# Attention scores in three memory banks used in turn by head, and a ring of four banks for everything else

## What is computed

```
x = x + 0.5 * attention(layernorm(x), W_gate, W_qkv)
x = x + recurrence(layernorm(layernorm(x)), ...)       # gates, a scan over time, W_out, W_skip
x = x + 0.5 * attention(layernorm(x), W_gate, W_qkv)   # the same weights again

attention: 2048 tokens, 256 features, 16 heads of 16
  every token picks one head for keys and values (argmax of the gate softmax):
  k_shared, v_shared [2048, 16]; all 16 query heads use them
  y = softmax(causal(q k_shared^T / 4)) v_shared
```

## Time and profile before

| | |
|---|---|
| median of three runs | 1090.59 us (1089.08 to 1090.8) |
| the profiled execution | 1086.89 us, span from first to last instruction 1085.2 us |
| PE / DVE / ACT / POOL busy | 990.2 / 820.7 / 751.6 / 267.3 us |
| granted TensorE clock, mean | 0.899 of full speed |
| exponentials (line 924) | 640, 594.5 us, 985 ns each on average |
| maxima (line 1050) | 960, 601.0 us, 683 ns each on average |

### The profile page before, as it was taken

One profiled execution on the slowest core, in us unless ns is written; L12 is line 12 of the kernel. 1 busy time (PEld: TensorE's weight loads), 2 busy tenths in 40 slices (PEclk: granted clock), 3 DMA queues, 4 the chain that ended last, 5 costly groups with the idle time before them and its releaser, 6 DMA issues. The chain is left out here.

```text
span 1085.2 us, 17469 instructions
## 1 busy us (share of the span) xinstructions
PE 990.2 (91%) x6546; PEld 335.9 (31%) x6546; DVE 820.7 (76%) x1448; ACT 751.6 (69%) x984; POOL 267.3 (25%) x497
## 2 busy tenths in 40 slices
PE   8897999989989899989998999989899989999986
PEld 6433332222332322223333342323242222222322
DVE  1676787798849798977864878877869898989731
ACT  2347467748667466877856867767838747888896
POOL 1226322221152201133123222521202210210324
PEclk9887599879999996989997989889989868999999
DMA  4110010000100100000010001000010000000000
GB/s 146 50 50 1 1 36 15 2 1 2 50 1 2 50 1 1 2 1 1 2 49 1 2 18 33 2 20 1 2 42 8 2 21 1 1 2 1 3 8 33
DMA packets 20228, 17.92 MB, mean 17 GB/s; under 512 B 4128, under 2 KB 20144, under 8 KB 20144
## 3 DMA queue, kind: packets, MB, share of 16 engines
q1 hardware_dynamic: 19328, 16.00, 4.8%
q10 hardware_dynamic: 816, 0.80, 0.2%
HBM read 10.24 MB, written 6.29 MB: 15 GB/s over the span
## 5 line engine op out<-in xcount | busy, mean ns | idle before, releaser
L1050 DVE TENSOR_REDUCE mxp<-ps_x 128x1 f32<-128x512 f32 (+2 forms) x960 | 601.0, 683 | 132.0 <-PE ps_x L1266 128.3
L924 ACT ACTIVATE probs<-ps_s,e_scale 128x1024 f32<-128x1024 f32 (+3 forms) x640 | 594.5, 985 | 142.3 <-PE ps_s L1289 138.8
L1266 PE MATMUL ps_x<-k_tl,q_t 48*128 48x512 f16 (+2 forms) x1792 | 346.3, 323 | 34.3 <-DVE mxp L1050 18.6
L1299 PE MATMUL ps_o<-probs,v_l 128*32 128x512 f32 (+3 forms) x2560 | 322.8, 581 | 6.3 <-POOL probs L737 5.0
L1289 PE MATMUL ps_s<-q_t,k_tl 50*128 50x512 f16 (+3 forms) x1280 | 269.1, 373 | 25.7 <-ACT probs L924 20.0
L1266 PEld LDWEIGHTS ps_x<-k_tl,q_t 48*128 48x128 f16 x1792 | 115.1, 99 | 316.2 <-DVE mxp L1050 228.2
L737 POOL TENSOR_SCALAR_AFFINE_SELECT probs<-probs 128x256 f32<-128x256 f32 x256 | 102.9, 410 | 228.4 <-ACT probs L924 227.6
L752 POOL TENSOR_SCALAR_AFFINE_SELECT d_sb<-d_sb 128x1024 f32<-128x1024 f32 x64 | 69.4, 1092 | 264.9 <-ACT d_sb L915 260.5
L1289 PEld LDWEIGHTS ps_s<-q_t,k_tl 50*128 50x128 f16 x1280 | 67.6, 96 | 185.7 <-ACT probs L924 141.5
L915 ACT ACTIVATE d_sb<-ps_x 128x512 f32<-128x512 f32 x128 | 71.0, 599 | 37.8 <-PE ps_x L1266 34.7
L1299 PEld LDWEIGHTS ps_o<-probs,v_l 128*32 128x32 f32 x2560 | 53.3, 111 | 101.4 <-issue 79.8
(11 more groups left out here) (111 smaller groups left out, 492.6 us busy)
## 6 DMA issues: line engine op xcount, KB each, us to landing
q_t<-q_scratch SPq DMA_DIRECT2D x96, 64.0 KB, 2.2
q_scratch<-q_part SPq DMA_DIRECT2D x16, 256.0 KB, 2.1
x_sb<-in_L_attn_x_dram SPq DMA_DIRECT2D x4, 512.0 KB, 8.6
out_dram<-x_sb SPq DMA_DIRECT2D x4, 512.0 KB, 2.9
q_t<-m_row SPq DMA_DIRECT2D x64, 4.0 KB
wqkv_n<-in_L_ffn_W_qkv_dram ACTq DMA_DIRECT2D x1, 768.0 KB, 6.5
w_in_sb<-in_L_attn_W_in_dram SPq DMA_DIRECT2D x1, 384.0 KB, 5.2
w_skip_sb<-in_L_attn_W_skip_dram SPq DMA_DIRECT2D x1, 256.0 KB, 4.6
```

Source lines behind the costliest of these rows:

```text
L924: a_.activation(probs[:, s % NB, 2 * hp:2 * hp + 2, P * i:QW], ps_s[hp][:, :, P * i:QW], ACT.Exp, scale=e_scale[:, 0:1]).then_inc(s_exp, 1)
L1050: v_.tensor_reduce(mxp[:, heads[0] % 2, h0:h1, tiles[0]:tiles[-1] + 1:i_step, slot], bank_of(e)[:, :].rearrange("p (h i k) -> p h i k", i= ...
L1266: last = mm(bank[:, col:col + w], q_rows(ROWS_X, c, g, hh, i * P, P), k_cols(ROWS_X, hh, l, key // P, w), start=True, stop=True)
L1299: last = mm(ps_o[VW * hh:VW * hh + VW, P * i:QW], v_l[:, l, kt, :], probs[:, s % NB, hh, P * i:QW], start=j == 0, stop=j == key_tiles(c) - 1)
```

## The change

- **Scores.** `ps_s` is one tile of three banks (`SB = 3`). Head `h` of step `s` uses bank `(4 s + h) mod 3`. A step has three score events and three exponentials: heads 0 and 1 together, then 2, then 3, and in every third step 0, then 1 and 2 together, then 3 (`GROUPS`), since a pair must lie in neighbouring banks. PE waits for the exponential of the head three before.
- **Ring.** `RING = 4`.
- **Exponential's scale.** Queries and keys are scaled so that the scale is the number `SCALE / LIFT ** 2`. The factors are now from the largest row norm of the weights: squares, two reductions, and a fourth root and two square roots on POOL (`roots`). `M_SCALE` goes from 256 to 32768.
- **Opening.** DVE copies the weight blocks out of PSUM in place of ACT, and computes the norms after the last of them. In `FIRST_WORK` the gate weights and the statistics come first, both turns of the first chunk stand ahead of `range`, and the gate product between the two `range` events.
- **Statistics.** DVE adds EPS and negates the mean; POOL has two instructions fewer.
- **Planner.** Two halves of the array are followed each for itself, side events depend on what they need in place of the last side event, costs are changed, and `SIDE_WORK` has other steps.
- POOL masks a diagonal step in three instructions in place of two.

```diff
-RING = 3
+RING = 4
-M_SCALE = 256.0
+M_SCALE = 32768.0
+IN_RANGE, LIFT = 40000.0, 0.125
+GROUPS = [[(0, 2), (2, 1), (3, 1)], [(0, 2), (2, 1), (3, 1)], [(0, 1), (1, 2), (3, 1)]]
+SB = 3
+PER_STEP = len(GROUPS[0])
+def group(s, k):
+    return GROUPS[s % SB][k]
-FIRST_WORK = [("weights", r) for r in range(6)] + [("wgate",)] + prepare(0, 0)
-FIRST_WORK[8:8] = [("range", 0), ("range", 1)]
-SIDE_WORK = [(-23, -10, prepare(0, 1)), (9, 9, [("bias",)]), (9, 40, prepare(0, 2)), (57, 57, prepare(0, 3)),
-             (60, 65, branch(0)), (81, 81, prepare(1, 0)), (117, 140, branch(1)), (140, 140, prepare(1, 1)),
-             (140, 158, branch(2)), (164, 174, prepare(1, 2)), (180, 203, branch(3)), (210, 214, prepare(1, 3))]
+FIRST_WORK = [("wgate",), ("stats", 0, 0)] + [("weights", r) for r in range(6)] \
+    + [("norm", 0, 0), ("turn", 0, 0, 0), ("turn", 0, 0, 1), ("range", 0), ("gate", 0, 0), ("range", 1)] \
+    + prepare(0, 0)[5:]
+SIDE_WORK = [(-38, -25, prepare(0, 1)), (10, 10, [("bias",)]), (10, 24, prepare(0, 2)), (57, 60, prepare(0, 3)),
+             (63, 63, branch(0)), (81, 84, prepare(1, 0)), (113, 140, branch(1)), (140, 140, prepare(1, 1)),
+             (140, 157, branch(2)), (165, 180, prepare(1, 2)), (180, 203, branch(3)), (210, 210, prepare(1, 3))]
-EXP, EXP_COLUMN = 150, 1.66
+EXP, EXP_COLUMN = 65, 0.83
...
-        if e[0] in SIDE_KINDS and e[0] not in ("kv", "q", "skip"):
-            t = max(t, self.side_end)
-        return t
+        return max([t] + [ended[x] + back for x in needs(e)])
...
-        ps_s = [pb(f"ps_s{i}", [P, 2, QW]) for i in range(2)]
+        ps_s = pb("ps_s", [P, SB, QW])
...
+        def scores_of(s, k):
+            first, heads = group(s, k)
+            at = (GH * s + first) % SB
+            return ps_s[:, at:at + heads, :]
...
-                    a_.activation(probs[:, s % NB, 2 * hp:2 * hp + 2, P * i:QW],
-                                  ps_s[hp][:, :, P * i:QW], ACT.Exp, scale=e_scale[:, 0:1]).then_inc(s_exp, 1)
+                    a_.activation(probs[:, s % NB, first:first + heads, P * i:QW], scores_of(s, k)[:, :, P * i:QW],
+                                  ACT.Exp, scale=SCALE / LIFT ** 2).then_inc(s_exp, 1)
...
+                v_.tensor_scalar(var[:, :], mv[:, :, 1], EPS, None, ALU.add)
+                v_.tensor_scalar(neg[:, :], mv[:, :, 0], -1.0, None, ALU.mult).then_inc(s_var, 1)
+            def loading(e):
+                r = e[1]
+                dve.wait_ge(s_fill, filled(e))
+                v_.tensor_copy(wqkv_t[:, :, r * P:(r + 1) * P],
+                               bank_of(e)[:, 0:DC * P].rearrange("p (a h) -> p a h", a=DC)).then_inc(s_rd, 1)
+                if r == 5:
+                    own(v_.tensor_tensor(squares, rows, rows, op=ALU.mult))
+                    own(v_.tensor_reduce(w_rows[:, :], squares, axis=AX, op=ALU.add))
+                    v_.tensor_reduce(w_part[:, :], w_rows[:, :].rearrange("p (a r) -> p a r", a=2), axis=AX,
+                                     op=ALU.max).then_inc(s_norms, 1)
...
+                    own(v_.tensor_copy(w_ratio[:, 1:3], bank[:, 0:2]))
+                    own(v_.reciprocal(w_inv[:, :], w_ratio[:, 1:3]))
+                    v_.tensor_tensor(w_ratio[:, 0:1], w_ratio[:, 1:2], w_inv[:, 1:2], op=ALU.mult)\
+                        .then_inc(s_norms, 1)
+                    dve.wait_ge(s_root, 1)
...
-                    if s:
-                        pe.wait_ge(s_exp, 2 * (s - 1) + hp + 1)
+                    past = GH * s + first + heads - 1 - SB
+                    if past >= 0:
+                        pe.wait_ge(s_exp, exp_of(past))
```

More of the change, by code:

```diff
@@ L157, in weights @@
     if e[0] == "max":
-        beside = e[2] % 2 and past == ("max", e[1], e[2] - 1)
-        return 15 if beside else 226, "rows", [("ACT", 480) if on_diagonal(e) else ("DVE", 600)]
+        return 226, "rows", [("ACT", 480) if on_diagonal(e) else ("DVE", 600)]
     if e[0] == "warm":
@@ L214, in run, with run2, use, ready @@
             t += d
-    def start(self, e):
+    def run2(self, t, work, use):
+        end = t + work / (1.0 if self.full else 0.5)
+        gain = max(0.0, end - max([t] + self.halves)) * (1.0 if self.full else 0.5)
+        self.streamed += gain
+        return end
+    def start(self, e):
+        t = self.ready(e)
+        if t is None:
+            return None
+        if e[0] in ("qk", "max"):
+            return max([t] + [self.halves[p] for p in self.use(e)])
+        return max([t] + self.halves) if weights(e, None)[0] else t
+    def use(self, e):
+        if e[0] == "qk":
+            first, heads = group(*e[1:])
+            return [h % 2 for h in range(first, first + heads)]
+        return [BANKS[UNITS[e[1]][1]][e[2]][2][0] % 2]
+    def ready(self, e):
         ended = self.ended
@@ L283, in place @@
         ended[e] = t
+        if e[0] == "qk":
+            first, heads = group(*e[1:])
+            for h in range(first, first + heads):
+                self.exps[4 * e[1] + h] = t
         self.said.append(e)
-        if e[0] in SIDE_KINDS and e[0] not in ("qout", "qin"):
-            self.side_end = t + TO_NEXT
 def weave():
@@ L305, in weave @@
         order.append(e)
-    scores = [("qk", s, hp) for s in range(len(STEPS)) for hp in range(2)]
+    scores = [("qk", s, hp) for s in range(len(STEPS)) for hp in range(3)]
     sums, maxima, ends, rows = [], [], [], []
@@ L404, in read_by_scalar @@
 def read_by_scalar(e):
-    return e[0] in ("weights", "wgate", "turn", "keys", "row", "skip") or (e[0] == "gates" and e[2] != 1) \
+    return e[0] in ("wgate", "turn", "keys", "row", "skip") or (e[0] == "gates" and e[2] != 1) \
         or on_diagonal(e)
@@ L425, with exp_no, exp_of @@
 TURNS = [_e for _e in ORDER if _e[0] == "turn" and _e[3] == DC - 1]
+def exp_no(s, k):
+    return PER_STEP * s + k + 1
+def exp_of(n):
+    return exp_no(n // GH, next(k for k in range(PER_STEP) if sum(group(n // GH, k)) > n % GH))
 def filled(e):
@@ L937, in _ @@
                     norm(e)
-                elif e[0] in ("weights", "wgate", "turn", "keys", "row"):
+                elif e[0] in ("wgate", "turn", "keys", "row"):
                     evict(e)
@@ L1197, in preparation @@
                     pe.wait_ge(s_ra, max(FREED["turn", l, c, 1], FREED["wgate",]))
+                    if kind != "gate" and prep_no(l, c) == 0:
+                        pe.wait_ge(s_rd, FREED["weights", 5])
                 if kind == "gate":
```

210 lines of the change are left out of this document (130 added, 80 removed).

## The result

The changed kernel takes 1097.74 us (median of six, 1096.52 to 1103.18), the kernel before 1089.84 in the same series: a ratio of 1.0082, 95 % interval 1.0058 to 1.0107. It is slower by 0.8 %, some 9 us, where I had forecast it 2 % faster. The forecast was 1068 us with a range of its own of 1045 to 1083; the measured time lies outside that range and inside the wide one, 1038 to 1108, which was drawn to take in the rivals.

A forecast was written before the change was run, and what follows sets the result against it. Bound: PE's one in-order list and how far each consumer's buffers carry it while PE serves the other. -6.5 - 9 + 5 + 13 - 25 = -22.5 us from 1086.9 gives 1064.4; median 3.7 above, 1068 us, range 1045 to 1083.

The forecast's parts named there:

- Opening, forecast -6.5: Start of the kernel: first maximum near 34.7 us in place of 41.2, -6.5 us, bounds 2 and 9 us gained.
- Exponentials, forecast -9: ACT's 320 steps: 0.11 us less each, 35 us in all, a quarter taken as path: -9 us, bounds 0 and -35.
- +5: Tail, three score banks: 9 wide steps 0.3 us longer, 12 narrow ones 0.2 each: +5 us, bounds -2 and +9.
- +13: Middle, three score banks: a third of 38 us (0.3 us on 128 last-chunk steps): +13 us, bounds 0 and 67.
- Order, forecast 0: Whole kernel: the planner's new costs and side steps reorder everything; put at 0, with 15 us to either side.
- Ring, forecast -25, at most -60: Fourth ring bank gives DVE 0.61 us more to read while PE is away: -25 us, bounds 0 and -60.
- The cap of 74 us: Most the fourth ring bank can take off: DVE's 122 waits for PE times 0.61 us.
- Third event, forecast no loss on PE: Score products on PE: two single-head loads cost nothing by themselves if a maximum's product of other parity stands beside them.
- Three score banks, forecast +18, bounds -2 and 76: One score bank fewer on ACT's side: refills come late, costing 5 us in the tail and 13 in the middle.
- the sign of being wrong: Steps of the last chunk's units taking over 2.5 us each, where they took 2.3 before.
- the three banks become the pace: Rival, slower: full 0.3 us on 128 steps (+38), tail +5, ring worth only 12: 1115 us, chance 0.24.
- not below 95: Sign of being right: DVE's wait for PE falls from 125 to below 95 us.

The follow-up runs named there:

- the held order: Opening, number as scale and statistics of the change on the kernel before, every event behind the opening in its old place: 1075.2 us, ratio 0.9867.
- the other order: Order of the all-but-banks kernel, planned anew with changed planner and side steps (1108.4 us); splitting only ACT's exponential of heads 2 and 3 there: 1125.0 us.

## Why the prediction was wrong

**Opening, forecast -6.5.** Right: the first maximum is 7.6 us early, and on a held order opening and scale together give 14.5. Planned anew by the old planner, nothing of it is left (1090.7 us).

**Exponentials, forecast -9.** Right in price (0.597 and 1.023 us). The size, 9 us with an interval of 5 to 13 on the old banks, is partly luck: I had counted a quarter of 35 us, and it is 17 % of the 52 us that the scale alone saves there. In the changed kernel ACT is busy 21 us less, not 35, and half of ACT's time is path. Splitting an exponential made ACT busy 19 us longer on the held order (716.9 against 698.3), 58 ns for each of 320, and the time did not rise. The Trainium skill ("VectorE: DVE Perf Modes", the section on the TRN2 errata) gives ScalarE 172 cycles for each instruction from PSUM, an estimated 143 ns; what it says of many small tiles it says of sources in SBUF. On the other order the split cost 14 us, for 18 us more of ACT. So the fixed part is there, smaller than by that table, and what it costs differs from order to order.

**The failed step is the term put at nothing: "The planner's new costs and side steps reorder everything; no row prices that. I put it at 0, with 15 us to either side".** With the old banks, pairs and ring, the new order alone takes 34 us (1.0175 against 0.9867): 16 when the old planner plans from the new opening, 18 for the changed planner. On top of that new plan, third event, banks and ring together give 10 us back (1.0175 to 1.0082). The forecast for them was "+5", "+13" and "-25", together -7, and the agreement is luck: measured one by one they are +49, +41 and -101. Together order, banks and ring are 1.0082 - 0.9867, +23 us, forecast -7.

| | between plans | on a held order |
|---|---|---|
| new plan from the new opening | +16 | |
| changed planner | +18 | |
| third event and exponential | +49 | +6, or +31 with the change's grouping (before's order) |
| fourth score bank away | +41, the change's grouping in it | +152 (before's order), 8 to 21 (changed order, ring of three) |
| fourth ring bank | -101 | -110 to -121 (changed order), -15 (before's order) |

- *Order, forecast 0.* It has no row in a profile, and I let it stand at zero with a range of 15. Side steps alone make 42 us in the changed kernel, the planner's model 16 to 18, the new opening seen by the same planner 16.
- *Ring, forecast -25, at most -60.* The sign was right, the size a fourth of the measured between plans. The cap of 74 us counted only DVE's own waits times 0.61. A ring bank that is not there stops PE, and with it the scores: under the changed order ACT's waits rose by 73 us, DVE's by 81, and the clock fell.
- *Third event, forecast no loss on PE.* On before's order it costs 6 us, with the change's grouping 31; the sum had no term for the grouping.
- *Three score banks, forecast +18, bounds -2 and 76.* The "+5" for the tail was near on before's order (52.0 to 57.5 us). The changed kernel's tail is 31 us longer for another reason: nine more steps are left when the maxima end, and each takes 2.50 us on average in place of 2.13, with the same waits when the fourth bank is given back. For the middle I took a third of 0.3 us on 128 steps, of which only 104 are wide. Between 900 and 1000 us the changed kernel does 111 exponentials, 37 steps, 2.70 us each; before, 84 or 42 steps, 2.38 each. That is over the 2.5 us that I had named as the sign of being wrong, though from 860 to 1000 us, with before's preparation in it, both do some 52. On before's order, with a ring of three, the bank away costs 152 us, twice the upper bound.

The rival that was nearest is "the three banks become the pace", at 1115 us, with its mechanism: ACT's wait for scores rose by more than 60 us (139 to 209, whole run). It had the order at 0 as well, and no run shows that the three banks set the pace: a fourth gave the changed order 8 to 21 us, and that with a ring of three. DVE's wait for PE fell only to 105, not below 95.

**What stays open.** How much of the changed kernel's +23 us is three banks and how much a plan that is merely unlucky can't be said, since each plan is one draw: prices of the same part differ by a factor of seven and more between orders. Four score banks with a ring of four, which would price the score bank in the changed kernel itself, need nine banks with `ps_o`. How much of a bank's price is waiting and how much the lower clock was not separated. What is shown is that opening and scale account for -14.5 and that all the rest together takes 23 back. Why the changed planner does worse than the old one with pairs was not tried further. The grouping's 25 us were measured with head 1's place fixed by me, not by a planner.

## What to carry to other kernels

When engines are fed from one in-order list, as here, a buffer has no price of its own: its worth depends on the order it meets (the same ring bank gave 110 to 121 us and 15, the same score bank 152 and 8 to 21). So change buffers and order in separate experiments, and hold the order while pricing a part: here that turned a change that lost 0.8 % into one that gains 1.3 %, by keeping its opening and its number as scale and leaving banks and order alone. When a plan is made anew, give it a term and a range of its own from a run that changes nothing but the plan. And count a stall of the shared engine for all that it feeds, not only for the one that owns the buffer.

## What the runs showed that I had not expected

The granted clock rose with the change while the time did too. From 750 to 1000 us it is 0.98 against 0.90, and 0.940 against 0.899 over the run, with PE busy 950 us in place of 990. The rise goes with the fourth ring bank: with a ring of three it is 0.905 under the same order and 0.869 planned anew. So what that bank gave the changed order may be in part faster matmuls. Neither the busy share nor the clock would have told that the kernel is slower.

Executions of a kernel scattered by more than two per cent after a small edit: the split exponential on the held order ran between 1065.6 and 1090.2 us, the kernel with the same order and no split between 1074.3 and 1079.5.
